# The statistics of the output's normalisation, from VectorE to ScalarE and GpSimd, in the first phase of a four-layer kernel

## The reference

```
h   = layernorm(x)
xz  = h @ in_proj_w ;  xb, z = split(xz)
xb  = silu(causal_conv(xb) + conv_b)
dt, b, c = from xb @ x_proj_w          (dt through softplus)
state_t = exp(dt_t * a) * state_{t-1} + dt_t * b_t * xb_t      16 states per channel
y_t = sum over states of state_t * c_t
out = ((y + D * xb) * silu(z)) @ out_proj_w
x   = x + (out - mean(out)) / sqrt(var(out) + 1e-5)            over the 128 channels
```

## Time and profile before

| | |
|---|---|
| time before, median of 3 runs | 2266.01 us (2258.45 to 2269.83) |
| the profiled execution | 2263.39 us |
| its span, first to last instruction | 2261.6 us |
| TensorE busy | 1885.6 us (83%) |
| VectorE busy | 1723.3 us (76%) |
| ScalarE busy | 1325.9 us (59%) |
| GpSimd busy | 855.5 us (38%) |
| mean granted clock of TensorE | 0.937 |

### The profile page before, as it was taken

The page is one execution under the profiler, slowest core; times in us unless marked ns, Lnnn a source line. Parts: engine busy times, 40 slices in busy tenths (PEclk is TensorE's granted clock), DMA queues, the critical chain, the costliest instruction groups (busy, mean ns, idle before and its releaser), DMA issues. The chain is left out here.

```text
span 2261.6 us, 38836 instructions
## 1 busy us (share of the span) xinstructions
PE 1885.6 (83%) x12576; PEld 1039.8 (46%) x12576; DVE 1723.3 (76%) x4299; ACT 1325.9 (59%) x2865; POOL 855.5 (38%) x710
## 2 busy tenths in 40 slices
PE   5888888866889989779627589999999999999975
PEld 2333333322444444334315246666656566666543
DVE  6999999984677777412266689899976899999875
ACT  5777777731444444234352368888873688888731
POOL 5787888841022222224421443333321333333211
PEclk8999999995999999789858789999999999999997
DMA  5333333203111111032260400000001000000011
GB/s 152 118 101 113 115 117 114 83 28 99 24 44 37 37 44 39 22 108 88 64 210 26 142 14 6 6 1 1 1 5 25 1 6 6 1 1 2 4 35 29
DMA packets 102297, 117.06 MB, mean 52 GB/s; under 512 B 27780, under 2 KB 78255, under 8 KB 101104
## 3 DMA queue, kind: packets, MB, share of 16 engines
q1 hardware_dynamic: 98000, 106.51, 15.9%
q0 software_dynamic: 4096, 8.06, 1.1%
HBM read 71.44 MB, written 38.11 MB: 48 GB/s over the span
## 5 line engine op out<-in xcount | busy, mean ns | idle before, releaser
L392 POOL TENSOR_TENSOR m_bu<-m_dtu,m_brow 128x1024 f32<-128x1024 f32 x128 | 299.7, 2356 | 56.6 <-DVE m_hs L816 54.7
L816 DVE TENSOR_TENSOR_SCAN m_hs<-m_ps_da,m_bu 128x1024 f32<-128x1024 f32 x128 | 292.4, 2284 | 3.6 <-POOL m_bu L392 2.5
L1361 ACT ACTIVATE a_pt<-a_ps_s 128x1024 f32<-128x1024 f32 x128 | 131.1, 1024 | 227.0 <-PE a_ps_s L1139 227.0
L2857 ACT ACTIVATE l_pe<-l_ps_s,l_nbias,l_qs 128x192 f32<-128x192 f32 (+1 forms) x512 | 244.4, 487 | 32.2 <-DVE l_nbias L3013 32.1
L521 PE MATMUL m_ps_y_ps<-m_prod,m_ident 128*128 128x512 f32 x512 | 243.8, 599 | 0.0
L1478 DVE TENSOR_REDUCE a_mpad<-a_ps_s 128x4 f32<-128x1024 f32 x128 | 156.9, 1226 | 92.3 <-PE a_ps_s L1131 91.1
L1131 PE MATMUL a_ps_s<-a_heads 32*128 32x256 f32 x1024 | 187.9, 447 | 43.1 <-DVE a_mpad L1478 28.5
L668 ACT ACTIVATE m_ps_da<-m_dt,m_a_neg 128x510 f32<-128x510 f32 x256 | 165.9, 681 | 75.9 <-DVE m_hs L816 75.2
L1139 PE MATMUL a_ps_s<-a_qm,a_heads 32*128 32x256 f32 x1024 | 185.6, 439 | 1.6 <-ACT a_pt L1361 1.2
L2629 PE MATMUL l_ps_s<-l_kT,l_qT 128*128 128x384 f32 (+1 forms) x512 | 179.9, 433 | 0.0
L2867 ACT COPY l_pT<-l_ps_t 128x256 f32<-128x256 f32 (+1 forms) x256 | 122.7, 479 | 72.8 <-PE l_ps_t L2639 46.0
(11 more groups left out here) (337 smaller groups left out, 4517.6 us busy)
## 6 DMA issues: line engine op xcount, KB each, us to landing
m_brow<-state_rows SPq DMA_DIRECT2D x64, 512.0 KB, 4.4
slots<-m_void SPq DMA_DIRECT2D x16, 516.0 KB, 5.4
e_xs<-slots SPq DMA_DIRECT2D x16, 258.0 KB, 2.7
ys<-m_void SPq DMA_DIRECT2D x8, 512.0 KB, 5.6
qk<-a_qk SPq DMA_DIRECT2D x16, 256.0 KB, 2.0
a_heads<-qk SPq DMA_DIRECT2D x64, 64.0 KB
ew_w<-in_w SPq DMA_DIRECT2D x2, 2048.0 KB, 12.4
e_yy<-ys SPq DMA_DIRECT2D x16, 256.0 KB, 5.3
```

Source lines behind the costliest of these rows:

```text
L392: nc.gpsimd.tensor_tensor(bu[s % 4][:, :, :], dtu[p][:, :, :], b2, ALU.mult).then_inc(bu_rd, 1)
L816: dve.tensor_tensor_scan(hs[s % 4][:, :, :].rearrange("p h t -> p (h t)"), da[s % 2][:, :, :, :].rearrange("p h q t -> p (h q t)"), bu[s % ...
L2857: nc.scalar.activation(pe_[u % 2][:, h, 0:nk], s_ps[u % 2][:, h * 192:h * 192 + nk], ACT.Exp, bias=nbias[:, u % 2, h:h + 1], scale=qs[b % ...
```

## The change

For all groups but the last one the two passes over the data that the statistics need are made by ScalarE. `copy_out` becomes four activations, one for each 128 tokens, that give the sum of each row beside the copy (`osum`). GpSimd scales the sums to minus the mean (`post_mean`, new). ScalarE squares the differences from the mean with the sums of the squares beside (`post_squares`, new; the squares themselves are written to `on` and not used). GpSimd scales these to the variance plus epsilon at the beginning of `post_rstd`. `post_norm` moves from step 3 to step 6, and in the last group the four steps for group 6 move to steps 7, 9, 10, 12 and 13. `post_stats` is left for group 7 alone.

```diff
                 def post_rstd(g):
-                    pool.wait_ge(ovar_ready, g + 1)
+                    if g < NG - 1:
+                        pool.wait_ge(osq_rd, g + 1)
+                        at_least(pool, out_rstd, g)
+                        nc.gpsimd.tensor_scalar(ove[:, :], osq[:, :], 1.0 / C, EPS, ALU.mult, ALU.add).then_inc(ove_rd, 1)
+                        pool.wait_ge(ove_rd, g + 1)
+                    else:
+                        pool.wait_ge(ovar_ready, 1)
+                def post_mean(g):
+                    pool.wait_ge(o_sb, g + 1)
+                    at_least(pool, orstd_ready, g)
+                    nc.gpsimd.tensor_scalar(onmean[:, :], osum[:, :], -1.0 / C, None, ALU.mult).then_inc(omean_rd, 1)
...
                         drive(g, p, s)
+                        if g > 1 and s == 0:
+                            post_mean(g - 2)
                         if g > 1 and s == 4:
                             post_rstd(g - 2)
...
-                            if s == 10:
+                            if s == 9:
+                                post_mean(g - 1)
+                            if s == 12:
                                 post_rstd(g - 1)
...
                 def copy_out(g):
                     act.wait_ge(out_mm, g + 1)
                     at_least(act, on_act, g)
-                    nc.scalar.copy(osb[:, :, :].rearrange("p c n -> p (c n)"), pr[:, :]).then_inc(o_sb, 1)
+                    at_least(act, omean_rd, g)
+                    for c in range(NCH):
+                        last = nc.scalar.activation(osb[:, c, :], pr[:, c * P:(c + 1) * P], ACT.Identity,
+                                                    accum_out=osum[:, c:c + 1])
+                    last.then_inc(o_sb, 1)
+                def post_squares(g):
+                    act.wait_ge(omean_rd, g + 1)
+                    at_least(act, ove_rd, g)
+                    at_least(act, on_rd, g)
+                    for c in range(NCH):
+                        last = nc.scalar.activation(on[:, c, :], osb[:, c, :], ACT.Square, bias=onmean[:, c:c + 1],
+                                                    accum_out=osq[:, c:c + 1])
+                    last.then_inc(osq_rd, 1)
...
-                        if s == 3 and g > 1:
+                        if s == 2 and g > 1:
+                            post_squares(g - 2)
+                        if s == 6 and g > 1:
                             post_norm(g - 2, kept)
...
-                            if s == 3:
+                            if s == 7:
                                 copy_out(g - 1)
-                            if s == 9:
+                            if s == 10:
+                                post_squares(g - 1)
+                            if s == 13:
                                 post_norm(g - 1, kept)
...
-                        if s == 1 and g > 1:
-                            post_stats(g - 2, kept)
-                        if g + 1 == NG and s == 5:
-                            post_stats(g - 1, kept)
```

More of the change, by code:

```diff
@@ L275, in phase_mamba @@
         onmean, shift_out = m.sb("onmean", [P, NCH]), m.sb("shift_out", [P, NCH])
+        osum, osq = m.sb("osum", [P, NCH]), m.sb("osq", [P, NCH])
         on = m.sb("on", [P, NCH, C])
@@ L298, in phase_mamba @@
         in_rstd, out_rstd = m.sem("in_rstd"), m.sem("out_rstd")
+        omean_rd, osq_rd, ove_rd = m.sem("omean_rd"), m.sem("osq_rd"), m.sem("ove_rd")
         NW = 8
@@ L833, in post_stats @@
                 def post_stats(g, src):
-                    post_own.turn(g)
-                    dve.wait_ge(o_sb if g < NG - 1 else out_mm, g + 1)
+                    dve.wait_ge(out_mm, g + 1)
                     for c in range(NCH):
@@ L851, in body @@
                 def body(g, p):
-                    kept = osb[:, :, :].rearrange("p c n -> p (c n)")
                     for s in range(NS):
```

## The result

The changed kernel takes 2298.85 us (median, 2294.36 to 2304.71), the kernel before 2263.97 us beside it: ratio 1.0156, 95% interval 1.0132 to 1.018. It is slower by 1.6%, 9.8 us more than the forecast of 2289 and just inside the upper end of the range. The profiled execution took 2294.91 us, with a span of 2293.1 us.

The account below looks back on a forecast made before the run. VectorE was taken to set the first phase's pace, TensorE close behind. Groups 2 to 6 add 5 x 4.9 = 24.5 us and group 7 0.5 to 2263.4, giving 2288.4; forecast 2289, range 2274 to 2300.

Parts of the forecast that it names:

- The first new wait: GpSimd's mean behind drive 0 waits for ScalarE's copy, delaying drive 1: scan 1 3.7 us late, scan 2 1.67.
- TensorE and its clock: TensorE idles 5.7 us before a group's first C row, so its clock falls to the lower level in every group.
- The price of 1.53: Cost of a clock fall in step 0: 5.78 us, as in group 1, instead of 4.25.
- rival (a): Same two waits, but TensorE's clock holds: 5 x 3.6 + 0.1 = 18.1 us more, 2281.5; chance 0.20.
- The second new wait: GpSimd's addition behind drive 8 waits for the normalisation behind decay 8: scan 9 4.9 us late with the clock's fall.
- Rival (b): Wait at the normalisation is covered, scan 9 late by VectorE's own 1.6 or 3 us; 2271.5 to 2279; chance 0.11.
- (d): Not slower: GpSimd's lead covers the mean; 2257.3 if the lead held in both places, or 2252.6; chance 0.04.
- One sign: VectorE's waits name the drive as releaser twice a group, about 3.7 us before scan 1, 1 to 2 before scan 9.
- Behind it the group runs at VectorE's pace, and the delay stays.: After scan 9's wait, the delay of 4.9 us stays to the group's end: 5 x 4.9 = 24.5 in groups 2 to 6.
- Rival (c): Costs more: clock stays low longer, copies at upper bound, 5 x 1.5 and 6 x 0.6 more, 2299.5; chance 0.10.
- What the removal alone would give: Statistics off VectorE: 0.6 us each in groups 2 to 6, 2 x 1.54 in group 7, together 6.1 us.
- What was covered: ScalarE's squares, about 1.8 us behind decay 4, are free; drive 5 is ready 2 us ahead of scan 5.

Follow-up runs that it names:

- five unread matmuls: Changed kernel plus five 128x512 matmuls whose result nothing reads, in TensorE's idle time at the start of groups 2 to 7; 2293.77 us, ratio 1.013.
- both: Changed kernel with GpSimd's mean behind drive 3 instead of 0 and its residual addition behind drive 13 instead of 8 (not in last group); 2257.28 us, ratio 0.9981.
- only ScalarE's work: Kernel before plus ScalarE's four-part copy with sums and four squares, results unread, statistics still on VectorE; 2262.54 us, ratio 1.0006.
- two unread matmuls: Changed kernel with mean at step 3, addition at step 13 and two matmuls nothing reads ahead of step 1's C row; 2250.97 us, ratio 0.995.
- no statistics: Kernel before with normalisation statistics left out for groups 0 to 6, constants used instead; 2260.31 us, ratio 0.9987.

## Why the prediction was right, and where not

**The first new wait: right in place, its size a little over.** GpSimd waits at the mean (8.2 us in group 2, where some 9 were expected; 6.65 in group 4, to which GpSimd comes later), drive 1 stands behind it, scan 1 is late: 3.0 us instead of 3.7, scan 2 0.9 instead of 1.67. The mis-sized term is the copy: the four activations start every 0.25 us, 1.0 us in all, where 1.80 was taken from the earlier trace rows and 0.59 was the lower bound. The Trainium skill ("ScalarE: Activation LUTs", What ACT_TABLE_LOAD costs) gives about 93 ns for each pointer operand; the prediction took one off, but the form of the earlier trace rows has two and the new copy names none in the profile. Two off make 1.80 - 4 x 2 x 0.093 = 1.06, an estimate by that page with which the measured 1.0 agrees.

**TensorE and its clock: right.** The idle time is 4.97 us instead of 5.7, less by what the copy was over. The clock falls with it in every one of groups 2 to 7, as the forecast took it, for 6.8 us. The price of 1.53 taken from group 1 measured 1.37 (five unread matmuls). So rival (a), in which the clock holds, is out. Scan 5 is 3.7 late, where the product there was put at 4.1.

**The second new wait: right.** The normalisation runs behind decay 8, GpSimd waits 8.2 us for it ("6" in the prediction's signs, but its own times give 298.6 + 1.63 - 292.4 = 7.8), and scan 9 is 4.2 late, forecast 4.9. Five groups: 21 us instead of 24.5. Rival (b), a covered second wait, is out, and so is (d): the mean's wait was real. One sign did not come: in groups 2 to 7 of the changed kernel no row names the drive as what a scan waited for. That it was the drive rests on the times above, on the mean's move, which takes the wait of scan 1 away and leaves a row of scan 9 that does name it, and on the addition's move, which takes the wait of scan 9 away.

**The step that failed: "Behind it the group runs at VectorE's pace, and the delay stays."** It looked at VectorE and at the drives and not at what else in GpSimd's list comes late behind the addition. The split for the next group does, ScalarE's cast waits for it, and decay 12 stands behind the cast. That is 2.95 us a group (7.11 at scan 14 less 4.16 at scan 9), 14.8 us in five, and the split's earlier place gave back 15.2 of the median, some 2 of them by the shorter falls of the clock. With the second wait's five groups 3.7 too high and group 1, whose clock happened not to fall in the profiled execution, 1.4 shorter, that is 14.8 - 3.7 - 1.4 = 9.7 of the 9.8 us by which the end of the first phase was missed; group 0, 0.6 longer, and group 7, 0.2 under its forecast, are left out. Rival (c) has nearly the measured time, 2299.5, but not by its mechanism: the clock did stay low for 6.8 us, but at a price of 1.4 us and not 3, and the copies took 1.0 us, far from their upper bound. That the measured time lies inside the range is luck: the range reached so far up for another cause.

**What the removal alone would give: too little.** The prediction expected 0.6 us a group, since TensorE would be next. At full clock it is 1.54, all of it: scan 5 gains only 0.8, but the waits for TensorE that the kernel before had ahead of scans 7 and 8, 0.25 and 0.23 us, go too, and at scan 8 the 1.54 are back. In "both", though, where TensorE's clock falls, 0.1 to 0.4 a group is left; the one group whose clock held gave 1.5 and group 7 gave 2.3. So that "both" met its 2258 is partly luck.

**What was covered** stayed so: the squares took 1.6 us, from 292.11, and drive 5 behind them was done at 295.38 + 2.3 = 297.7, four us ahead of its scan at 301.79.

## What to carry to other kernels

When work is moved to another engine, follow every list in which something now waits: the instruction that waits, those behind it on its engine, then whatever other engines want from those, until a lead is found that covers it. The same work, at the same prices, was 1.6% slower or 0.2% faster by where two small instructions stood in a list that runs in order. The engine that looked half idle had room for all of it; what was missing was an order in which its results were due after they were ready.

## What the runs showed of the hardware

An idle time of TensorE of 4.9 us or more came with a fall of the clock each time, in groups 2 to 7 of the changed kernel and of those with the addition or the split alone moved. One of 2.53 us was not so plain, with one profiled execution of each kernel: a fall in one of groups 1 to 7 of the kernel before, in six with both edits and in six without statistics, in two with the mean alone moved and in two with only ScalarE's work. With two unread matmuls, which left 0.82 us, there was none in groups 2 to 7. What decides at 2.53 us is open.

What a fall costs depends on what else is late. With the statistics off VectorE it made a group 1.4 us longer, in "both" and in "no statistics". With them on VectorE it cost nothing: group 2 of "only ScalarE's work" had the fall and took 57.88 us; the same group before had none and took 57.90. So the gain of the move and the price of the fall hide each other. In the kernel with five unread matmuls the clock fell later, 42 us behind scan 0, in groups 2, 4 and 5, and these were no longer than groups 3 and 6. The two matmuls were not tried in the kernel before, whose clock did not fall there in groups 2 to 7, so what 0.995 owes to the edits and what to them was not measured on that side.

A wait of several semaphores was put down to "issue" at scan 1 and to the decay at scan 9, where by time the drive ended last; with the mean moved, the same wait of scan 9 carried the drive's name.
